# A compressed interaction network on one core: 53 coefficient columns by quarters, two units to a block

## What is computed

```python
X = stack([tbl_f[ids[:, f]] for f in range(32)])          # (512, 32, 64)
x1 = einsum('oc,bcd->bod', W0, X (x) X) + b0              # 128 outputs from 32 * 32 products
x2 = einsum('oc,bcd->bod', W1, X (x) x1) + b1             # 128 outputs from 32 * 128 products
z  = concatenate([x1.sum(2), x2.sum(2)])                  # (512, 256)
h  = relu([z, dense_ctx] @ W_top1 + b_top1)               # 512
h  = relu(h @ W_top2 + b_top2)                            # 256
y  = h @ W_top3
```

## Time and profile before

| | |
|---|---|
| median of the runs | 245.91 us |
| the profiled execution | 247.0 us |
| its span, first to last instruction | 245.1 us |
| mean granted TensorE clock | 0.958 |
| PE, ACT, POOL, DVE busy | 212.4, 154.1, 147.0, 139.9 us |
| instructions | 11179 |

### The profile page before, as it was taken

The page is one execution under the profiler, slowest core; times in us unless marked ns, Lnnn a source line. Parts: engine busy times, 40 slices in busy tenths (PEclk is TensorE's granted clock), DMA queues, the critical chain, the costliest instruction groups (busy, mean ns, idle before and its releaser), DMA issues.

```text
span 245.1 us, 11179 instructions
## 1 busy us (share of the span) xinstructions
PE 212.4 (87%) x5033; PEld 179.3 (73%) x5033; DVE 139.9 (57%) x243; ACT 154.1 (63%) x386; POOL 147.0 (60%) x134
## 2 busy tenths in 40 slices
PE   7999995786999998999969696898868878698986
PEld 7788873775888776788858585688656767588784
DVE  1367599056888897764356567319384747652000
ACT  2689798594489788657574756367747474644043
POOL 4777789887877778877778878877786000000000
PEclk9999998597999999999997999999999799979999
DMA  6911117111111111111111111111111000000000
GB/s 185 337 33 24 27 19 274 23 25 27 27 27 29 27 25 27 24 24 32 29 24 25 29 26 26 24 29 24 29 24 29 5 3 3 4 5 3 3 0 3
DMA packets 6369, 9.60 MB, mean 39 GB/s; under 512 B 2705, under 2 KB 3089, under 8 KB 6322
## 3 DMA queue, kind: packets, MB, share of 16 engines
q0 software_dynamic: 4096, 4.20, 9.6%
q1 hardware_dynamic: 2082, 4.62, 5.7%
q10 hardware_dynamic: 144, 0.07, 0.1%
HBM read 8.87 MB, written 0.00 MB: 36 GB/s over the span
## 4 chain that ended last, share of the span: by engine, by line
PE 59%; issue 15%; ACT 10%; POOL 10%; DMA 5%; DVE 1%; ACTq 0%; DVEq 0%
PE psum L386 27%; PE psum L215 15%; POOL rows L513 10%; DMA rows<-table,idx 4%; PE psum L448 4%; ACT xx L259 3%; ACT t_sb L248 3%; PE psum L466 3%; PE psum L357 3%; PE psum L437 2%; PE psum L401 2%; PE psum L201 2%; ACT prod L267 2%; DMA t_sb<-ids 1%; PE psum L483 1%
## 5 line engine op out<-in xcount | busy, mean ns | idle before, releaser
L513 POOL DMA_INDIRECT rows<-table,idx x128 | 146.3, 1143 | 40.7 <-issue 38.7
L248 ACT ACTIVATE t_sb<-psum 64x308 f32<-64x308 f32 x196 | 82.5, 421 | 43.1 <-PE psum L215 39.8
L275 DVE TENSOR_TENSOR prod<-xx 128x1024 f32<-128x1024 f32 x64 | 75.6, 1223 | 16.1 <-ACT xx L259 13.9
L386 PE MATMUL psum<-coef,t_sb 128*32 128x128 f32 x2208 | 74.2, 282 | 3.8 <-issue 3.7
L386 PEld LDWEIGHTS psum<-coef,t_sb 128*32 128x32 f32 x2208 | 65.2, 114 | 9.5 <-issue 9.1
L215 PE MATMUL psum<-prod,xx 64*32 64x154 f32 x2048 | 46.0, 305 | 19.6 <-issue 16.0
L244 DVE COPY t_sb<-psum 64x308 f32<-64x308 f32 x60 | 28.8, 479 | 43.6 <-PE psum L215 43.1
L215 PEld LDWEIGHTS psum<-prod,xx 64*32 64x32 f32 x2048 | 34.0, 108 | 26.8 <-issue 22.7
L581 ACT ACTIVATE coef<-psum 128x256 f32<-128x256 f32 (+2 forms) x41 | 16.5, 481 | 6.6 <-PE psum L357 4.6
L259 ACT ACTIVATE xx<-psum 128x512 f32<-128x512 f32 x32 | 18.3, 597 | 1.0 <-PE psum L201 0.8
L581 ACT ACTIVATE t_sb<-psum 128x276 f32<-128x276 f32 x24 | 13.6, 669 | 7.1 <-PE psum L296 7.1
(11 more groups left out here) (36 smaller groups left out, 135.5 us busy)
## 6 DMA issues: line engine op xcount, KB each, us to landing
rows<-table,idx POOLq DMA_INDIRECT x128
w_sb<-w1t SPq DMA_DIRECT2D x3, 512.0 KB, 6.8
w_sb<-top SPq DMA_DIRECT2D x2, 512.0 KB, 4.7
t_sb<-w0x SPq DMA_DIRECT2D x1, 512.0 KB, 8.9
w0x_sb<-w0g SPq DMA_DIRECT2D x1, 512.0 KB, 3.4
w_sb<-w1t SPq DMA_DIRECT2D x1, 384.0 KB, 5.1
t_sb<-w0p SPq DMA_DIRECT2D x1, 276.0 KB, 2.9
w_sb<-w1t SPq DMA_DIRECT2D x1, 128.0 KB, 2.8
```

The source lines that it names most:

```text
L248: copy_t(act, lambda o, i: act.activation(o, i, ACT.Copy), 0, u, v)
L275: dve.tensor_tensor(at(p, e * COLS, [[2 * COLS, SUB], [HALF, SHIFTS], [1, HALF]]), at(x, x0, [[M, SUB], [0, SHIFTS], [1, HALF]]), at(x, x0 ...
L386: return pe.matmul(bank(UNIT_ACC[u % 2], n * O, O, UNIT * j, UNIT), t_sb[:, c:c + UNIT], w, start=start, stop=stop, tile_position=(0, UNIT ...
L513: pool.indirect_dma_start(rows[:, c:c + D], None, table[:, :], bass.IndirectOffsetOnAxis(ap=idx[:, g:g + 1], axis=0))\
```

## The change

- The fields are taken by quarters of 8. Of each quarter 36 pairs are formed (`NEAR`: products of its two fours, inside them, squares and neighbours) and 32 pairs of one quarter with the other of its half (`FAR`). Five DVE operations a half unit form them, with XT in PSUM as the first operand and xx as the second. xx keeps the fields once, 256 elements a half unit instead of 512; the gram is copied from xx.
- Of the 32 far columns each partition block needs half. Four DMAs a block on SP's queue (`pack`) move 16 of them from one half of the fields' partitions to the other, so that 53 coefficient columns remain instead of 69.
- The contraction takes blocks of two units, 64 samples wide on two places; units 14 and 15 are blocks of their own. There is one accumulator bank; `copy_acc` goes to ACT but for the last two.
- Rows are transposed by half units into two banks, with one semaphore a half for the gathers. On PE the transposes, and on ACT xx and gram, of half g of unit u+1 stand ahead of the factors and copies of half g of unit u, up to unit 11; from there the order is written out.
- W1 times W0 goes by slots, 40 in six steps: 212 columns a field for pairs, 192 near and 128 far for cross terms, all copied by ACT. The fold runs in twelve steps (63 operations for 40) as the slots come, and all coefficient transposes wait for its end. The far cross terms are read from parts of the near ones' W0 data.
- Unit 0's factors use matmuls of 77 columns, 64 records a group instead of 32.
- w0g has a buffer of its own and is loaded at the start; the weights of the top layers are loaded in pieces at units 3 to 6, and top1d and dense are padded to 128 partitions.

```diff
+QUART = HALF // 2
+GRAM = QUART
+OUTER, INNER, SQUARE, NEXT = 0, 16, 24, 32
+NEAR = QUART * (QUART + 1) // 2
+FAR = HALF
+PAIRS = NEAR + 2 * FAR
 COLS = PAIRS + GRAM + 1
-VCOLS = PAIRS + 1
+VCOLS = NEAR + 1 + FAR
+WIDE_Z = HALF + QUART
...
+BLOCKS = [(u, 2) for u in range(0, ALL - 2, 2)] + [(ALL - 2, 1), (ALL - 1, 1)]
...
+        XT = (0, 6)
+        ACC = 1
...
+        SLOTS = [(n, 2) for n in range(0, M, 2)]
+        STEPS_W = (("near", 0), ("near", 1), ("far", 0), ("far", 1), ("near", 2), ("near", 3))
+        for kind, n in STEPS_W:
+            SLOTS += [(QUART * n + x, 2) for x in range(0, QUART, 2)] if kind == "near" else [(HALF * n + x, 4) for x in range(0, HALF, 4)]
...
+            return int(p == 1 and (group % 2 == 1 if 8 <= group < 4 * (ALL - 1) else group < 8 or group % 4 > 1))
...
+        def transpose_rows(pe, u, g):
+
+            pe.wait_ge(gathered[u % UNITS][g], 16 * TILES // 2 * (u // UNITS + 1))
+            for ready in (xx_ready, prod_ready):
+                wait(pe, ready, 2 * (u - 1) + g + 1)
...
+        def narrow_group(pe, u, v):
...
+                        y = (4 * j + 2 * k + e) * COLS
+                        for r in range(2):
+                            last = pe.matmul(bank(TG + 2 * (v % 2) + r, n * COLS, COLS, 32 * (2 * e + k), M),
+                                             xx[u % 2][D * r:D * (r + 1), x:x + M],
+                                             p[D * r:D * (r + 1), y:y + COLS], start=True, stop=True)
...
+            x0 = g * SUB // 2 * M
+            act.activation(xx[u % 2][:, x0:x0 + SUB // 2 * M], bank(XT[g], 0, SUB // 2 * M), ACT.Copy).then_inc(xx_ready, 1)
...
+            act.wait_ge(xx_ready, 2 * u + g + 1)
...
-            for e in range(2):
-                dve.tensor_tensor(at(p, e * COLS, [[2 * COLS, SUB], [HALF, SHIFTS], [1, HALF]]),
-                                  at(x, x0, [[M, SUB], [0, SHIFTS], [1, HALF]]),
-                                  at(x, x0 + SHIFTS * e, [[M, SUB], [1, SHIFTS], [1, HALF]]), ALU.mult)
-            dve.tensor_tensor(at(p, SHIFTS * HALF, [[2 * COLS, SUB], [COLS, 2], [1, LAST]]),
-                              at(x, x0, [[M, SUB], [LAST, 2], [1, LAST]]),
-                              at(x, x0 + HALF // 2, [[M, SUB], [LAST, 2], [1, LAST]]), ALU.mult)\
-                .then_inc(prod_ready, 1)
+            def pairs(col, out, first, a, second, b):
+                return dve.tensor_tensor(at(p, col, out), at(psum, XT[g] * BANK + a, first), at(x, x0 + b, second), ALU.mult)
+
+            pairs(OUTER, [[COLS, 2 * SUB], [4, 4], [1, 4]], [[QUART, 2 * SUB], [1, 4], [0, 4]], 0,
+                  [[QUART, 2 * SUB], [0, 4], [1, 4]], 4)
+            pairs(INNER, [[COLS, 2 * SUB], [4, 2], [2, 2], [1, 2]], [[QUART, 2 * SUB], [4, 2], [1, 2], [0, 2]], 0,
+                  [[QUART, 2 * SUB], [4, 2], [0, 2], [1, 2]], 2)
+            pairs(SQUARE, [[COLS, 2 * SUB], [1, QUART]], [[QUART, 2 * SUB], [1, QUART]], 0,
+                  [[QUART, 2 * SUB], [1, QUART]], 0)
+            pairs(NEXT, [[COLS, 2 * SUB], [1, 4]], [[QUART, 2 * SUB], [2, 4]], 0, [[QUART, 2 * SUB], [2, 4]], 1)
+            pairs(NEAR, [[COLS, 2 * SUB], [1, 2 * FAR]], [[HALF, SUB], [1, QUART], [0, QUART]], 0,
+                  [[HALF, SUB], [0, QUART], [1, QUART]], QUART).then_inc(prod_ready, 1)
...
+                add(OUTER, [(4, 4), (1, 4)], *((4, 0, (YS, XS)) if second else (0, 4, (XS, YS))))
+                for m in (0, 4):
+                    add(INNER + m, [(2, 2), (1, 2)], *((m + 2, m, (YS, XS)) if second else (m, m + 2, (XS, YS))))
+                last = add(NEXT, [(1, 4)], *((1, 0) if second else (0, 1)), (2 * XS + 2 * YS,))
+                if not second:
+                    last = add(SQUARE, [(1, QUART)], 0, 0, (XS + YS,))
...
+            if n == 0:
+                pe.wait_ge(fold_step, FOLD_ALL)
...
+        def pack(sp, b):
+
+            u, units = BLOCKS[b]
+            for n in range(2):
+                wait(sp, t_copied[n], copied(n, 4 * (u + units)))
+            for e in range(2):
+                for k in range(2):
+                    dims = [[CHUNK, FAR], [1, units * UNIT]]
+                    c, p = t_at(u) + NEAR * CHUNK, 2 * M * e + HALF * (1 - k)
+                    sp.dma_start(at(t_sb, c, dims, p + M * (1 - k), HALF),
+                                 at(t_sb, c + FAR * CHUNK, dims, p + M * k, HALF)).then_inc(packed[b], 16)
...
+                pe.wait_ge(packed[b], 4 * 16)
+            for i in range(PARTS[part], PARTS[part + 1]):
+                last = contract_tile(pe, b, i, VCOLS, 1, T_COL[i], coef[:, i * O:(i + 1) * O])
...
+        def contract_tile(pe, b, i, n, half, col, w):
+            u, units = BLOCKS[b]
+            width = units * UNIT
+            places = 128 // width
+            c, j = t_at(u) + col * CHUNK, i % places * width
+            return pe.matmul(bank(ACC, half * O, O, j, width), t_sb[:, c:c + width], w,
+                             start=i < places, stop=i >= n - places, tile_position=(0, j))
...
+        def copy_acc(eng, copy, b):
+
+            eng.wait_ge(block_done, b + 1)
+            wait(eng, z_done, b - 1)
+            copy(acc_sb[b % 2][:, :], bank(ACC, 0, 2 * O)).then_inc(acc_copied, 1)
...
+            pack(sp, 0)
+            sp.wait_ge(t_done, 4 * 3)
+            sp.dma_start(w1_sb[:, top1_at:top1_at + TOP1], top1[:, 0:TOP1]).then_inc(top_in_sb, 16)
+            sp.wait_ge(t_done, 4 * 4)
+            sp.dma_start(w1_sb[:, top1_at + TOP1:top1_at + 2 * TOP1], top1[:, TOP1:2 * TOP1]).then_inc(top_in_sb, 16)
+            pack(sp, 1)
...
+            for b in range(2, len(BLOCKS)):
+                pack(sp, b)
...
+            t_half(pe, 1, 0)
+            t_half(pe, 1, 1)
+            for u in range(2, EVEN):
+                b = u // 2 - 1
                 for g in range(2):
-                    t_group(pe, u, 2 * g)
+                    if b == 0:
+                        contract(pe, b, 2 * (u % 2) + g)
+                    if u < EVEN - 1:
+                        transpose_rows(pe, u + 1, g)
+                    t_half(pe, u, g)
+                    if u == EVEN - 1:
+                        transpose_rows(pe, u + 1, g)
+                    if b > 0:
+                        contract(pe, b, 2 * (u % 2) + g)
+                    if g == 0 and top_step(u, 7) is not None:
+                        l1(pe, top_step(u, 7))
+                    if g == 1 and top_step(u, 7) is not None:
+                        l2(pe, top_step(u, 7))
+                    if g == 0 and top_step(u, 8) is not None:
+                        l3(pe, top_step(u, 8))
+                if u % 2 == 0 and b >= 1:
+                    sum_z(pe, b - 1)
...
+            t_half(pe, 12, 0)
+            l3(pe, 1)
+            contract(pe, 5, 0)
+            transpose_rows(pe, 13, 0)
+            sum_z(pe, 4)
+            t_half(pe, 12, 1)
+            contract(pe, 5, 1)
+            contract(pe, 5, 2)
+            transpose_rows(pe, 13, 1)
+            t_half(pe, 13, 0)
+            contract(pe, 5, 3)
+            transpose_rows(pe, 14, 0)
+            sum_z(pe, 5)
+            t_half(pe, 13, 1)
+            l1(pe, 2)
+            transpose_rows(pe, 14, 1)
+            t_half(pe, 14, 0)
+            contract(pe, 6, 0)
+            contract(pe, 6, 1)
+            transpose_rows(pe, 15, 0)
+            t_half(pe, 14, 1)
+            contract(pe, 6, 2)
+            transpose_rows(pe, 15, 1)
+            contract(pe, 6, 3)
+            t_half(pe, 15, 0)
             for part in range(4):
-                unit_cin(pe, ALL - 1, part)
-                if part == 1:
-                    sum_z(pe, ALL - 2)
-            l1(pe, END - 1)
-            sum_z(pe, ALL - 1)
-            l2(pe, END - 1)
-            l1(pe, END)
-            l3(pe, END - 1)
-            l2(pe, END)
-            l3(pe, END)
+                contract(pe, 7, part)
+            t_half(pe, 15, 1)
+            sum_z(pe, 6)
+            l2(pe, 2)
+            contract(pe, 8, 0)
+            contract(pe, 8, 1)
+            sum_z(pe, 7)
+            contract(pe, 8, 2)
+            l3(pe, 2)
+            contract(pe, 8, 3)
+            sum_z(pe, 8)
+            l1(pe, 3)
+            l2(pe, 3)
+            l3(pe, 3)
...
+                if u % 2 == 0 and u >= 4:
+                    copy_acc(act, plain, u // 2 - 2)
                 for g in range(2):
-                    act_copy_t(act, u, 2 * g)
-                    act_copy_t(act, u, 2 * g + 1)
-                    if 2 < u + 1 < LATE:
...
+                    if u < EVEN - 1:
+                        fields_in(u + 1, g)
+                        copies(u, g)
+                    else:
+                        copies(u, g)
+                        fields_in(u + 1, g)
...
+            for v in range(4):
+                dve_copy_t(dve, 1, v)
+            products(dve, 2, 0)
+            products(dve, 2, 1)
+
+            for u in range(2, ALL - 1):
                 for g in range(2):
```

(45 more changed lines are left out.)

604 lines of the change are left out of this document (317 added, 287 removed).

## The result

The changed kernel takes 196.27 us (median of 6 runs, 195.75 to 199.76) against 245.91 (6 runs): a ratio of 0.7987, 95% interval 0.7939 to 0.8035. Some runs of a kernel show a lower granted clock than its others and take over 1.5% longer than its fastest (here the one of 199.76, at 0.983); a ratio goes by the faster runs alone, a median by all. Its profiled execution took 196.0 us with a span of 194.2, at a mean granted clock of 0.991. The forecast was 204, so the direction held and the point was 8 us too high.

A forecast was written before the change was run, and what follows sets the result against it. PE bounded the early loop, a latency chain the late one, with gathers stretched by 25.3 us. Unit 11 at 137, 61.8 of PE work, 2.5 for gaps and 1.5 for packing gave 203 of span, plus 0.8: 204 us, range 196 to 226.

The forecast's parts named there:

- 64-wide record: PE's contraction: price follows width, so a record of 64 columns takes 0.061 us, bounds 0.030 to 0.124.
- products of a half, PSUM operand: DVE in the loop: five operations with one PSUM operand take 2.8 us per half unit, at most 5.0.
- fold's stretch of gathers: POOL beside DVE's fold of cross terms: gathers lengthened by 9 us in all, bounds 0 and 15.
- unit 1's factors: End of the work before the loop: PE starts these factors at about 53 us instead of 57.96.
- The 7 us that the errata section: DVE products: a higher fixed cost from PSUM would add some 7 us at the end; left out.
- The 15.6 us under the products: POOL in the loop: gather stretch beside DVE's products, 15.6 us, taken as gone; bounds 0 and 15.6.
- waits between its steps in which POOL gets in: New fold on DVE: pauses that let gathers through, given for taking 9 us of stretch where scaling gave 13.
- rows landed only at 174.3: Last gather: starts at 171.3, ends at 172.2, its rows land about 2.1 us later, at 174.3.
- 4% of gaps: Loop, units 4 to 10: 7.5 us a unit plus 4% gives 7.8, together 54.6 us.
- the coupling rival: Loop: dearer 64-wide records or engines waiting on each other; one extra us a unit gives 216, two 230; chance 20%.
- The bare sum of PE's terms: From unit 11's factors to the end: PE's work in order, 61.8 us, before any allowance.
- The 4 us of allowance for gaps and packing: Added from unit 11 to the end: 2.5 us for gaps, 1.5 for packing of the last two units.

The follow-up runs named there:

- c1: Changed kernel with both operands of DVE's products read from SBUF (xx) instead of one from PSUM: 216.91 us, ratio 0.8717.
- c2: Changed kernel with 69 coefficient columns in place of 53 and no packing DMAs (sum not right, for time only): 206.64 us, ratio 0.8349.
- d1: Changed kernel with 32 gathers in place of 128, later units reusing the rows of the first four: 195.24 us, no ratio given.
- e1: Kernel before with LATE = 16, so rows are transposed ahead in the late units too: 232.4 us, ratio 0.951.
- e2: Kernel before with LATE = 16 and products reading one operand from its single PSUM bank of transposed rows: 240.32 us, ratio 0.9813.

## Why the prediction was right, and where its 8 us went

The two steps that the forecast rests on held: the gathers' stretch beside the products went with the PSUM operand (c1), and PE, with fewer columns, sets the time nearly all along (c2, d1).

The 50.9 us of span, in runs: 15.5 are the late units' latency (the kernel before to e1; 12 by the ratio). Of the other 35.4, rows for the last half unit come 20.7 us earlier (190.80 to 170.13; c1 gives 21.4 for the PSUM operand alone), and from those transposes to the end it is 24.1 us instead of 38.8, for a shorter contraction and fewer units left after the rows; no run takes this second part apart into its causes, and on the old kernel the PSUM operand alone cost time (e2). These gains overlap with PE's work: were the contraction still 69 columns wide, 10.7 would be lost again (c2).

| step | predicted | measured |
|---|---|---|
| 64-wide record | 0.061 us (0.030 to 0.124) | 0.063 by the group, 0.055 in a row |
| products of a half, PSUM operand | 2.8 us (to 5.0) | 2.68 |
| xx, gram | 417 each | 386, 438 ns |
| fold | 15.7 us | 15.8 |
| fold's stretch of gathers | 9 us (0 to 15) | 1.6 |
| last gather starts | 171.3 | 164.40 |
| unit 1's factors | 53 | 50.75 |
| unit 4's factors | 76 | 72.89 |
| unit 11's factors | 137 | 131.81 |
| from there to the end | 66 (61.8 + 2.5 + 1.5) | 62.4 |

- **Products.** Right. The fixed cost with a PSUM source stays at some 145 ns: 256 elements at 1.046 are 268 of the 414, and in c1 the same operation from SBUF takes 419. The 7 us that the errata section of the Trainium skill (VectorE: DVE Perf Modes) would have added, by the prediction's estimate, were rightly left out; the run shows no surcharge.
- **Gathers.** The 15.6 us under the products went to nothing, as taken. The term that was mis-sized is the fold's: 9 us taken, from 9.7 scaled to 13 and cut, and 1.6 measured. ("Only the fold" has two SBUF operands left was nearly so: L840, with 0.7 us, is another.) Two things were wrong in it. First, the step read the gather of 6.72 us at 34.35 as the fold's; but the fold's row ends at 35.24, and products and the next fold steps follow in DVE's timeline. In e2, where the products read PSUM and the fold is the old one, the five slow gathers around it (1.57, 1.05, 1.70, 3.45 and 2.91 us) hold 6.0 us of stretch, so some 3.7 of the 9.7 were the products' and went with them. Second, the new fold, 15.8 us in 63 operations with hardly a pause, stretches the gathers by less than the old one of 11.7 us in 40 does. The prediction's "waits between its steps in which POOL gets in" has something in the trace for it, but not as a size. A merged row of DVE's timeline hides its breaks. Inside a row an operation mostly starts 0.08 to 0.09 us before the record of the one before ends; twice in the old fold (32.04 and 40.28) and six times in the new one (24.91, 27.68, 32.77, 35.30, 38.38, 41.00) it starts 0.04 us after. The old fold around its second break, and the new one around its third:

```profile
37.61 2.63 DVE L326 TENSOR_TENSOR t_sb<-t_sb,coef 128x1024 f32<-128x1024 f32 x4
40.28 3.19 DVE L326 TENSOR_TENSOR t_sb<-t_sb,coef 128x192 f32<-128x192 f32 x16
```

```profile
31.52 1.21 DVE L358 TENSOR_TENSOR t_sb<-t_sb,coef 128x1024 f32<-128x1024 f32 x1
32.77 2.50 DVE L358 TENSOR_TENSOR t_sb<-t_sb,coef 128x512 f32<-128x512 f32 x4
```

The gather of 6.72 us ends at 41.07, 0.83 behind the first of these; that of 1.24 at 32.32 ends at 33.56, 0.83 behind the second. The other gathers of over 2 us, in the kernel before, e2 and c1, also end 0.81 to 0.83 us behind such a break or the end of the fold. That the extra breaks are why the new fold stretches less is read from this; no run adds or removes one. The size matters for the measured kernel: with rows landed only at 174.3, its transposes at 170.13 would have waited 4 us.
- **Before the loop.** 2.3 us too many: the 256 records of unit 0 took 4.05 us and a gap, near the 5.1, but the 53 transposes behind them were through 6.2 us after the factors, not 8. Another 0.8 came off between unit 1's factors and unit 4's.
- **The loop.** 58.9 us instead of 61 from unit 4 to 11. I took 4% of gaps over the engines' sums; PE had 0.4%. DVE was busy for 44.4 and ACT for 42.4 of the 50.45 us, so neither was level with PE, and their waits didn't add to it: the coupling rival (20%) did not occur.
- **The end.** The bare sum of PE's terms was 61.8 us, the trace has 62.4. The 4 us of allowance for gaps and packing were the error.

The misses are 2.3 + 0.8 + 2.1 + 3.6 = 8.8 us of span, all of one sign. The last two, 5.7 us, are allowances for something that might go wrong, added to a sum of terms that rows had given; the first two are terms of the ramp taken too long. The fold's term, the largest that was off, is in none of them: the forecast had PE at unit 15's second half at 176, behind rows landed at 174.3, so an error of 7 us in the rows didn't reach the sum. That was luck of the path, not of the term.

## What to carry to other kernels

Here a DVE product with one operand in PSUM cost the same as one with both in SBUF and left the gathers alone, but it keeps that bank busy for longer: give the operand a second bank, or the wait moves to PE (18.7 us in e2). Don't read a bound from the chain's shares where several engines are level; take the work away and time it. In a point forecast put in the terms that rows show, and keep allowances for the range.

## What was not expected of the hardware

The granted clock fell for about 4 us in the loop of the changed kernel, after PE had stood for 1.95 us before the transposes of unit 4. Two windows of it, columns as above:

```profile
72.30:76.30 4.00, 4.00 (x82) 2.98 (x84) 3.92 (x8) 3.29 (x9) 3.09 (x4) 0.58 0.42 83
76.30:80.30 4.00, 4.00 (x110) 3.42 (x108) 3.73 (x9) 2.46 (x7) 3.09 (x4) 1.00 0.32 57
```

At a granted 0.58, most of that time at the lower level (1.2 GHz), 64 records of L220 took 2.30 us against 1.43 in the kernel with fewer gathers, where the same pause (1.96 us) came at nearly the same time and the clock stayed up. It puts PE 1.3 us further behind that kernel, and the trace doesn't show why the one fell and the other didn't. Over the whole kernel it can't be seen: the changed kernel's run at a granted 1.000 took 196.06 us, those at 0.991 took 195.75 to 196.48.
